# A recommendation tower on one NeuronCore: top layers in pairs of units, last two units spread in parts, identity matmuls in TensorE's pauses

## The reference

```python
xk = x
for i in range(3):
    z = einsum('bfe,bge->bfge', x, xk).reshape(B, F*F, E)      # pairwise products
    z = einsum('bcl,oc->bol', swapaxes(z, 1, 2), Ws[i]) + bs[i][None, :, None]
    z = sum(relu(z), axis=-1)                                  # (B, 16)
    outs.append(z)
    xk = broadcast_to(z[:, :, None], (B, F, E))
h = concatenate(outs + [dense_ctx], axis=1)                    # (512, 64)
h = maximum(h @ W_top1 + b_top1, 0)                            # 512 wide
h = maximum(h @ W_top2 + b_top2, 0)                            # 256 wide
y = h @ W_top3
```

## Time and profile before

| | us |
|---|---|
| median of 3 runs | 172.34 |
| lowest and highest | 171.52, 172.9 |
| the profiled execution | 171.46 |
| its span | 169.6 |
| busy in the span: VectorE (DVE) | 144.9 |
| TensorE matmuls (PE), weight loads (PEld) | 137.1, 92.4 |
| ScalarE (ACT), GpSimd (POOL) | 126.3, 121.0 |

### The profile page before, as it was taken

One profiled execution on the slowest core, in us unless ns is written; L12 is line 12 of the kernel. 1 busy time (PEld: TensorE's weight loads), 2 busy tenths in 40 slices (PEclk: granted clock), 3 DMA queues, 4 the chain that ended last, 5 costly groups with the idle time before them and its releaser, 6 DMA issues.

```text
span 169.6 us, 6453 instructions
## 1 busy us (share of the span) xinstructions
PE 137.1 (81%) x2728; PEld 92.4 (54%) x2728; DVE 144.9 (85%) x136; ACT 126.3 (74%) x441; POOL 121.0 (71%) x84
## 2 busy tenths in 40 slices
PE   0045998988887878787879797999898999993995
PEld 0024665746464646464646464757474876763963
DVE  3169986999999999999999999999999998198330
ACT  3020465586979797979797979798999998977461
POOL 1777989898888888888888888989797995000000
PEclk9999999999999999999999999999999999999599
DMA  2343653131313030303030303031313100000000
GB/s 56 94 123 97 190 151 97 30 98 37 93 33 95 25 101 12 112 9 117 2 114 10 103 20 103 24 99 35 96 32 97 31 4 4 6 0 2 4 0 0
DMA packets 5273, 9.98 MB, mean 59 GB/s; under 512 B 2179, under 2 KB 2947, under 8 KB 5252
## 3 DMA queue, kind: packets, MB, share of 16 engines
q0 software_dynamic: 3072, 8.39, 17.2%
q1 hardware_dynamic: 2036, 1.29, 2.8%
q10 hardware_dynamic: 144, 0.00, 0.0%
HBM read 9.68 MB, written 0.00 MB: 57 GB/s over the span
## 4 chain that ended last, share of the span: by engine, by line
PE 46%; DVE 19%; ACT 18%; issue 8%; POOL 4%; DMA 3%; DVEq 1%; ACTq 0%
PE Y L627 25%; DVE PR L311 13%; ACT prod L387 8%; ACT XT L357 7%; PE T L592 5%; POOL X L329 4%; PE T L688 4%; PE ZB L648 4%; DVE prod L503 3%; PE Y L633 2%; ACT Y L378 2%; PE YD L670 2%; DMA X<-in_table,idx 2%; PE YD L688 2%; PE YD L604 1%
## 5 line engine op out<-in xcount | busy, mean ns | idle before, releaser
L311 DVE TENSOR_TENSOR PR<-T,XT 128x1024 f32<-128x1024 f32 (+2 forms) x72 | 101.1, 1450 | 7.0 <-ACT XT L357 6.9
L627 PE MATMUL Y<-PR,w_sb 128*32 128x272 f32 x1024 | 66.0, 399 | 13.0 <-DVE PR L311 12.6
L329 POOL DMA_INDIRECT X<-in_table,idx x64 | 61.2, 956 | 20.7 <-issue 16.1
L387 ACT ACTIVATE prod<-prod,bias_sb 128x256 f32<-128x256 f32 x122 | 60.1, 498 | 4.2 <-DVE prod L503 4.2
L311 POOL TENSOR_TENSOR PR<-XT 128x2048 f32<-128x2048 f32 (+2 forms) x16 | 59.7, 3734 | 0.3
L627 PEld LDWEIGHTS Y<-PR,w_sb 128*32 128x32 f32 x1024 | 31.1, 110 | 35.7 <-issue 12.1
L503 DVE TENSOR_TENSOR prod<-U,ZB 128x2048 f32<-128x2048 f32 (+1 forms) x18 | 35.6, 1982 | 3.4 <-PE ZB L648 3.3
L378 ACT ACTIVATE Y<-Y,bias 128x136 f32<-128x136 f32 x64 | 21.5, 336 | 14.2 <-PE Y L633 14.2
L592 PE MATMUL T<-ident_sb,X 128*128 128x128 f32 x128 | 21.7, 314 | 12.3 <-DMA X<-in_table,idx 12.3
L357 ACT ACTIVATE XT<-T 128x1024 f32<-128x1024 f32 (+1 forms) x17 | 16.6, 974 | 18.1 <-PE T L592 13.2
L592 PEld LDWEIGHTS T<-ident_sb,X 128*128 128x128 f32 x128 | 17.5, 211 | 14.0 <-issue 9.9
(11 more groups left out here) (48 smaller groups left out, 69.3 us busy)
## 6 DMA issues: line engine op xcount, KB each, us to landing
X<-in_table,idx POOLq DMA_INDIRECT x64, 2.8
w_sb<-in_w SPq DMA_DIRECT2D x1, 512.0 KB
w_sb<-in_w SPq DMA_DIRECT2D x1, 224.0 KB
sel_sb<-in_sel SPq DMA_DIRECT2D x1, 128.0 KB
ident_sb<-in_ident SPq DMA_DIRECT2D x1, 64.0 KB, 2.1
w1l_sb<-in_w1l SPq DMA_DIRECT2D x1, 64.0 KB
w2l_sb<-in_w2l SPq DMA_DIRECT2D x1, 64.0 KB
w_sb<-in_w SPq DMA_DIRECT2D x1, 64.0 KB
```

Source lines behind the costliest of these rows:

```text
L311: return eng.tensor_tensor(pr, x0.broadcast_to(shape), x1.broadcast_to(shape), ALU.mult)
L329: pool.indirect_dma_start(out=X[:, n % NV, g, :], out_offset=None, in_=table, in_offset=bass.IndirectOffsetOnAxis(ap=idx[:, NT * n + g:NT ...
L387: last = act.activation(q, q, ACT.Relu, bias=bias_sb[:, l + 1:l + 2], accum_out=to)
L627: pe.matmul(Y[TR * j:TR * j + TR, h, 0:YC], w0_sb[:, c, :], PR[:, v, h, c, CB * j:CB * (j + 1), :].rearrange("q b s -> q (b s)"), start=c ...
```

## The change

- **Tower.** CHUNKS becomes six chunks of 2 units and one of 4. Of the first five, one starts at every odd step from 5 on: SP copies the three layers' sums into a small buffer `pair` when ScalarE has made them; step 5 + 2k on TensorE selects pair k and does the second hidden layer of pair k - 1 (tower_select), step 6 + 2k does the output of pair k - 1 and the first hidden layer of pair k (tower_hidden). Both stand between the transposes and layer_u. The loop now covers steps 7 to 14. The first bias becomes a row of the weights, so that one ScalarE instruction evacuates a whole first hidden layer.
- **Head.** Unit 0 and unit 1 are taken in halves: contract(0, h) starts when half h has its products, and the second half of unit 1 is transposed between the two contractions. 10, 8 and 4 matmuls of the identity by itself (keep_busy) stand in front of the transposes of unit 0, behind them and behind the first transposes of unit 1.
- **Products.** GpSimd takes 4 rows in unit 14 (6 before) and all 8 in unit 15 (6 before).
- **Tail.** Three buffers of prod instead of two. Units 14 and 15 have their spread and outer product in five pieces (PIECES), two of the spreads inside the last contractions. Two half stages are folded by GpSimd from 256 to 64 numbers, one of them after a relu by ScalarE, and VectorE reduces them. TensorE multiplies the identity by itself 4, 12 and 5 times.

The core of the diff:

```diff
-POOL_ROWS = {0: 0, NU - 2: 6, NU - 1: 6}
-TAIL_SHARE = {(NU - 2, 0): 2, (NU - 1, 0): 2, (NU, 1): 2}
-LOOP = range(3, 11)
...
+POOL_ROWS = {0: 0, NU - 1: 8}
+STAGES = [(s, l) for s in range(NU + 1) for l in range(2) if 0 <= s - l < NU]
+ACT_SHARE = {(NU - 2, 0): 2, (NU - 1, 1): 2, (NU, 1): 2, (NU - 3, 1): 0, (NU - 2, 1): 0}
+FOLDS = [(NU - 3, 1), (NU - 2, 1)]
+DVE_SUMS = [(NU - 2, 0), (NU - 1, 1), (NU, 1)]
+ACT_SUMS = STAGES[:STAGES.index((NU - 4, 0))] + [
+    (NU - 4, 0), (NU - 3, 0), (NU - 2, 0), (NU - 4, 1), (NU - 1, 0), (NU - 1, 1), (NU, 1)]
+PIECES = [(NU - 2, 0), (NU - 2, 1), (NU - 1, 0), (NU - 1, 1), (NU, None)]
+PIECE_BLOCKS = [(0, SB), (SB, 2 * SB), (0, CB), (CB, 2 * SB), (SB, 2 * SB)]
+CHUNKS = [(0, 2), (2, 4), (4, 6), (6, 8), (8, 10), (10, 12), (12, 16)]
+LAST = len(CHUNKS) - 1
+FIRST = 5
+PW = 2 * UB
+LOOP = range(FIRST + 2, NU - 1)
...
+            for k in range(LAST - 1):
+                sp.wait_ge(z0_ready, 2 * CHUNKS[k][1])
+                wait_sums(sp, (CHUNKS[k][1], 1))
+                wait(sp, selected, k)
+                for l, src in enumerate(sums_of(*CHUNKS[k])):
+                    sp.dma_start(pair[:, l, :, :], src).then_inc(paired, 16)
...
+            pool.wait_ge(bias_in, 16)
+            step = 0
+            for s, l in FOLDS:
+                b0 = act_share((s, l))
+                q = prod[:, s % NPR, SB * l + b0:SB * (l + 1), :, :].rearrange("q b f g -> q b (f g)")
+                if (s, l) == FOLDS[0]:
+                    pool.wait_ge(prod_ready, outer_done((s, l)))
+                    pool.tensor_scalar(q, q, bias_sb[:, l + 1:l + 2], 0.0, ALU.add, ALU.max)\
+                        .then_inc(pool_step, 1)
+                    step += 1
+                    pool.wait_ge(pool_step, step)
+                else:
+                    pool.wait_ge(relu_ready, FOLDS.index((s, l)))
+                pool.tensor_tensor(q[:, :, 0:P], q[:, :, 0:P], q[:, :, P:2 * P], ALU.add)\
+                    .then_inc(pool_step, 1)
+                step += 1
+                pool.wait_ge(pool_step, step)
+                pool.tensor_tensor(q[:, :, 0:P // 2], q[:, :, 0:P // 2], q[:, :, P // 2:P], ALU.add)\
+                    .then_inc(folded, 1)
...
+            def tower_select(n, k):
+                pe.wait_ge(u_read, n)
+                first = k if isinstance(k, int) else 1
+                if first == 0:
+                    pe.wait_ge(weights_in, 16 * 5)
+                    pe.wait_ge(dense_in, 16)
+                if first >= 1:
+                    pe.wait_ge(h1_ready, k)
+                if not isinstance(k, int) or in_flow(k):
+                    pe.wait_ge(paired, 16 * 3 * (k + 1))
+                    select_chunk(selected_psum(0), [pair[:, l, :, :] for l in range(3)])
+                if first >= 1:
+                    for c in range(HC2):
+                        second_hidden(k - 1, c)
+            def tower_hidden(n, k):
+                pe.wait_ge(u_read, n)
+                pe.wait_ge(h_ready, k + 1)
+                wait(pe, h2_ready, HC2 * k)
+                if not isinstance(k, int) or k >= 1:
+                    outputs(k - 1)
+                first_hidden(k, slice(PW * k, PW * (k + 1)) if isinstance(k, int)
+                             else bass.ds(PW * k, PW))
+            def keep_busy(to, count):
+                for _ in range(count):
+                    pe.matmul(to, ident_sb[:], ident_sb[:], start=True, stop=True)
             pe.wait_ge(ident_in, 16)
+            keep_busy(ZB[:, 2 * P:3 * P], 10)
...
+            keep_busy(ZB[:, 2 * P:3 * P], 8)
             pe.wait_ge(consts_in, 16 * 5)
             pe.wait_ge(minus_half_ready, 1)
+            pe.matmul(mask_g_ps, ident_sb[:], mask_g_sb[:], start=True, stop=True).then_inc(mask_ready, 1)
+            transpose(1, 1, 0, (0,))
+            keep_busy(ZB[:, 2 * P:3 * P], 4)
+            contract(0, 0, 0)
+            transpose(1, 1, 0, (1,))
+            layer_u(0, 0)
+            contract(0, 0, 1)
+            transpose(2, 0, 1)
+            layer_u(1, 1)
...
+            layer_u(NU - 1, last, (0,))
+            contract(NU - 2, 1 - last, 0)
+            spread_rows(NU - 3)
+            contract(NU - 2, 1 - last, 1)
+            contract(NU - 1, last, 0, [(NU - 2, 0)])
+            contract(NU - 1, last, 1, [(NU - 2, 1), (NU - 1, 0)])
+            layer_u(NU - 1, last, (1,))
+            keep_busy(T_bank[1][1][:, 2 * P:3 * P], 4)
+            spread_rows(NU - 1, 1)
+            pe.wait_ge(h1_ready, LAST - 1)
+            for c in range(HC2):
+                second_hidden(LAST - 2, c)
+            keep_busy(T_bank[1][1][:, 2 * P:3 * P], 12)
             spread_rows(NU)
+            pe.wait_ge(u_read, NU + 1)
+            pe.wait_ge(h2_ready, HC2 * (LAST - 1))
+            wait_sums(pe, (NU - 4, 1))
+            select_chunk(selected_psum(LAST - 1), sums_of(*CHUNKS[LAST - 1]))
+            outputs(LAST - 2)
+            pe.wait_ge(h_ready, LAST)
+            first_hidden(LAST - 1, samples(LAST - 1))
+            n0, n1 = CHUNKS[LAST]
+            to = selected_psum(LAST)
+            select(to, 0, zz[:, n0:n1, 0:SB])
+            wait_sums(pe, (NU - 1, 0))
+            select(to, 1, zz[:, n0 + 1:n1 + 1, SB:2 * SB])
+            keep_busy(T_bank[1][1][:, 2 * P:3 * P], 5)
+            for half in STAGES:
+                if half[1] == 1 and half[0] > n0:
+                    wait_sums(pe, half)
+            select(to, 2, z2[:, n0:n1, :]).then_inc(selected, 1)
```

More of the change, by code:

```diff
@@ L10 @@
 ACT = mybir.ActivationFunctionType
+AX = mybir.AxisListType
 ALU = mybir.AluOpType
@@ L19 @@
 NV = 2
+NPR = 3
 EH = 64
@@ L625, in contract @@
                 for c in range(NC):
+                    if c >= NC - len(spreads):
+                        spread_rows(*spreads[c - NC])
                     for j in range(NJ):
@@ L697, in _, with select_chunk, first_hidden @@
-            pe.wait_ge(ident_in, 16)
+            def select_chunk(to, layers):
+                for l, src in enumerate(layers):
+                    last = select(to, l, src)
+                last.then_inc(selected, 1)
+            def first_hidden(k, cols):
+                w = 0 if not isinstance(k, int) else k
+                per = HC1 // len(hidden1_psum(w))
+                for c in range(HC1):
+                    pe.matmul(hidden1_psum(w)[c // per][:, c % per, :], w1_sb[:, c * P:(c + 1) * P],
+                              H[:, cols], start=True, stop=True).then_inc(hidden1, 1)
@@ new lines, in second_hidden, with outputs @@
+            def second_hidden(k, c):
+                w = 0 if not isinstance(k, int) else k
+                for q in range(HC1):
+                    last = pe.matmul(hidden2_psum(w, c), w2_sb[:, q, c * P:(c + 1) * P], h1_of(w, q),
+                                     start=q == 0, stop=q == HC1 - 1)
+                last.then_inc(hidden2, 1)
+            def outputs(k):
+                w = 0 if not isinstance(k, int) else k
+                for q in range(HC2):
+                    last = pe.matmul(output_psum(w), w3_sb[:, q:q + 1], h2_of(w, q), start=q == 0,
+                                     stop=q == HC2 - 1)
+                last.then_inc(output, 1)
@@ L736, in _ @@
-            contract(NU - 1, last, 1)
-            for done in MLP_STEPS[NU - 1]:
-                wait_sbuf(pe, done)
-            pe.wait_ge(u_read, NU)
-            for c in range(HC1):
-                tower((1, HIDDEN1, c))
-            spread_rows(NU - 1)
-            n0 = CHUNKS[2][0]
-            select(2, 0, n0, NU)
-            select(2, 1, n0, NU - 1)
-            select(2, 2, n0, NU - 2)
-            tower((1, HIDDEN2, 0))
-            spread_rows(NU)
-            tower((1, HIDDEN2, 1))
```

591 lines of the change are left out of this document (308 added, 283 removed).

## The result

The changed kernel takes 181.45 us (median of four runs, 178.91 to 183.39), the kernel before 172.31: a ratio of 1.049 (95% interval 1.044 to 1.055). The forecast was 174.4, with a range up to 177.4. The direction was right, the size was not. The ratio leaves out runs more than 1.5% above the fastest of their kernel, here the one of 183.39; the medians alone give 1.053. The profiled execution is the shortest of the four, 178.91 with a span of 177.1, against a sum of 173.5 on that scale: 5.4 too little. The forecast also had no place for the spread of the changed kernel's runs.

What follows compares the result with a forecast made beforehand. VectorE bound the kernel before; with the tower in pairs TensorE would (18.1 against 17.04 a pair). Unit 15 3.9 later (+3.6 loop, +0.4 copies, +1.1 products, -1.2 head), tail -1.9: 173.5 profiled, 174.4 as median, range 169.1 to 177.4.

Steps and rivals of the forecast that it cites:

- The load as the floor of a pass: Tower on TensorE: any pass with 128 weight columns costs 0.112 us, a select pass 0.031, set by loading weights.
- the weight load hides: Rival, chance 0.20: tower passes of 64 columns take 0.06, a pair needs 16.9, VectorE stays the bound; 169.1 us.
- Given back exactly: Rival, chance 0.27: shape changes cost nothing, select passes 0.028, odd steps 9.9, even 7.9; 172.4 us, no change.
- A step without tower costs TensorE 6.73: Unit step: 9.43 us read in step 14 of the kernel before, less 2.70 of tower.
- SP's copies at 0.1 a pair: Loop: the select's wait for SP's small copies, 0.1 for each of four, 0.4 us; bounds nothing and 0.5 a pair.
- 1.2 won in the head: Head: contracting by halves, less the identity matmuls' cost, wins 1.2 us; upper end 2.6, lower end -0.7.
- the head's identities cost more than the reorder wins: Rival, chance 0.15: at half rate they make units 2 onward start 0.7 later instead of 1.2 earlier; 176.3 us.
- The tail at 30.6: Tail: from VectorE's start of unit 15 to the end takes 30.6 us, 1.9 less than the 32.5 before.
- If it falls all the same, 1.6 comes back: Tail: should TensorE's clock drop to half as before, the 1.6 us counted as saved is lost again.
- I take the clock as full throughout: Tail: TensorE's clock never halves; before, three us at half clock cost 1.6, counted as saved.
- The alternating step: Sign of being right: the unit step alternates between about 8.5 and 9.6 us, VectorE waiting for XT every second one.
- A tail above 32 us from unit 15: Sign of being wrong: more than 32 us from unit 15, where 30.6 was forecast.

Runs made afterwards that it cites:

- the fours: Changed kernel with TensorE's loop written out, SP's copies gone and the tower on chunks of four units instead of two: 169.37 us, ratio 0.983 to the kernel before.
- direct kernel: Changed kernel with TensorE's hardware loop unrolled and the select reading ScalarE's sums itself, without SP's copies: 177.17 us, ratio 1.031 to the kernel before.
- written-out kernel: Changed kernel with TensorE's hardware loop over steps 7 to 14 unrolled, SP's copies kept: 183.13 us, ratio 1.057 to the kernel before.
- fourth group: Last set of follow-up runs, on one chip; the changed kernel was run there again unaltered: 180.74 us, ratio 1.050 to the kernel before.

## Why the prediction was wrong in size

- **The load as the floor of a pass: right.** Sixteen second-hidden passes take 1.93 (forecast 1.8), the select 1.41 (1.5), odd tower work 3.35 (3.4), even 1.35 (1.25); and the fours show it directly. The rival "the weight load hides" falls, and with it a loop in which VectorE stays the bound. "Given back exactly", with its even cheaper steps, falls too: its pair was 17.8.
- **"A step without tower costs TensorE 6.73": the step that failed first.** It was read off step 14 of the kernel before, which stands behind the hardware loop there. In the changed kernel it is 6.98 and 7.00, and inside the loop every second step has 0.37 to 0.44 more at the branch, which the sum had nowhere. 2 x 0.26 + 0.4 is the 0.9 by which the pair of 18.1 fell short of 19.0; over the three and a half pairs between unit 8 and 15 that makes the loop's 3.0. The direct kernel (18.5 a pair, no branch and no copy) bears out the branch's share. Its steps without tower still take 6.8 to 7.0, so 6.73 is too low even without the loop.
- **SP's copies at 0.1 a pair: right in the profiled run** (0.23 at most), wrong as a bound. The written-out kernel waits 2.1 in four pairs. The bounds of nothing and 0.5 a pair held a pause for its length alone; with the spell behind it the pair with the wait of 1.06 is 2.5 longer than at full clock, 1.4 beyond the wait. The pair with a spell and no wait is 1.7 longer, so the spell has a price of its own that the sum held nowhere.
- **1.2 won in the head: wrong, 0.2.** The forecast took the products as the last thing to wait for. The start of unit 3 hangs on GpSimd's gather, which starts where it did, and in the profiled run up to 0.3 of it is the spell at 32; the 2.3 won at unit 2 became a wait of 2.24 at unit 3. The rival "the head's identities cost more than the reorder wins" falls as well: without them it is no faster (1.2 slower by the medians).
- **The tail at 30.6: right at full clock** (30.6 to 30.7 in five profiles with this tail, one of them the changed kernel's in the fourth group), 32.1 where a spell lies in it. "If it falls all the same, 1.6 comes back" is what happened.
- **"I take the clock as full throughout": wrong, and as large a mistake as the loop.** I priced the 21 identities as a cost alone. Without them the tail is 33.5, 1.4 more than with them in the profiled run and 2.9 more than at full clock. And a kernel whose TensorE is late in every step passes a half-clock spell in the loop on in full, 2.0 to 2.2 here; the runs have one to four. Of the 7.0 us between forecast and median, 5.4 are in the profiled run (head 1.0, loop 3.0, tail 1.5), and 1.6 come because the median lies 2.5 above that run, where I took 0.9 from the kernel before. Head and loop alone would have put the forecast at 178.4, outside the range already; the tail's spell and the further ones of the median make the rest.
- **What would show it.** The alternating step came, TensorE waited for no product behind 68.65, and VectorE stood in every pair, though it waits for the spread (1.26 to 1.56) more than for XT (0.28). "A tail above 32 us from unit 15" was named as a sign of being wrong, and is what came.
- GpSimd's folding, taken at nothing, cost nothing: its first instruction took 3.70 and the folds were done at 156.69 and 159.66, but VectorE reached its two reductions at 159.27 and 163.34.

## What to carry to other kernels

Where one engine is behind in every step, read its step from the very loop in question, branch included, and look at what smaller pieces do to its fixed price per instruction: here sixteen weight loads served 64 samples as dearly as 128, and a tower in fours, with the loop written out and the copies gone, turned a ratio of 1.03 into 0.98. Before counting on time won at one unit, follow it to the next wait that has another source (here a gather whose issue had not moved). And where TensorE is the late engine, count its half-clock spells by place, in several profiles: the mean clock alone does not tell their price. Filler work has to be tried both ways: the same five matmuls were neutral in the tail of one version and cost 1.1 in the next.
